# A fused decoder layer on one core: the turn of the attention output one sequence later, and two new orders at the ends of stages

## The reference

```python
x = x + attn(layernorm(x), W_qkv)                 # one head, causal
x = x + xattn(layernorm(x), ctx, mask, Wq..bo)    # 16 heads of 8, softmax over 128 keys
x = x + ffn(layernorm(x), w_gate, w_up, w_down)   # hidden width 384
# act_qdq(t): scale = max(|t|) / 32767 over the WHOLE tensor, t = round(t / scale) * scale
# ffn: x = act_qdq(x); up = act_qdq(x @ dq(w_up).T); gate = act_qdq(x @ dq(w_gate).T)
#      gate = act_qdq(gate * fixed_qdq_u16(sigmoid(gate))); o = act_qdq(gate * up)
#      return o @ dq(w_down).T                    # dq: weights at 4 bits in blocks of 32
```

## Time and profile before

| | us |
|---|---|
| median of 3 runs (lowest, highest) | 330.36 (329.21, 331.45) |
| the profiled execution: its time | 329.18 |
| the same execution: span of the trace | 327.4 |
| PE busy, share of the span | 303.7 (93%) |
| DVE | 273.6 (84%) |
| ACT | 255.3 (78%) |
| POOL | 191.2 (58%) |

### The profile page before, as it was taken

The page is one execution under the profiler, slowest core; times in us unless marked ns, Lnnn a source line. Parts: engine busy times, 40 slices in busy tenths (PEclk is TensorE's granted clock), DMA queues, the critical chain, the costliest instruction groups (busy, mean ns, idle before and its releaser), DMA issues.

```text
span 327.4 us, 9964 instructions
## 1 busy us (share of the span) xinstructions
PE 303.7 (93%) x3757; PEld 208.7 (64%) x3757; DVE 273.6 (84%) x652; ACT 255.3 (78%) x470; POOL 191.2 (58%) x339
## 2 busy tenths in 40 slices
PE   6999999997999999999999998999966689697996
PEld 5787877886566666666666666844322254357996
DVE  5489988777888989999999975877789996989754
ACT  3578888986798998899899896797787758992940
POOL 3679999971348797866857578100077773781000
PEclk9999999999999999999999999999999999999999
DMA  6941366642203565500000000000000000000134
GB/s 167 292 124 33 99 207 194 206 129 72 68 2 100 161 183 163 149 2 6 4 3 4 3 4 2 1 0 0 2 0 1 0 1 2 0 0 1 36 98 126
DMA packets 23754, 21.65 MB, mean 66 GB/s; under 512 B 3577, under 2 KB 21530, under 8 KB 23706
## 3 DMA queue, kind: packets, MB, share of 16 engines
q1 hardware_dynamic: 22170, 20.73, 21.0%
q10 hardware_dynamic: 1536, 0.28, 0.5%
HBM read 14.70 MB, written 6.30 MB: 64 GB/s over the span
## 4 chain that ended last, share of the span: by engine, by line
PE 66%; DVE 11%; ACT 9%; POOL 6%; issue 4%; DMA 2%; SPq 1%; POOLq 0%; ACTq 0%; DVEq 0%
PE banks L772 11%; PE banks L716 9%; PE banks L992 8%; DVE mxs L1823 7%; PE banks L1062 7%; PE banks L646 4%; PE banks L794 4%; PE banks L785 3%; PE banks L639 3%; ACT ng L1358 3%; PE banks L790 3%; PE banks L725 2%; POOL rstd L380 2%; PE banks L709 2%; PE banks L658 2%
## 5 line engine op out<-in xcount | busy, mean ns | idle before, releaser
L1597 DVE TENSOR_REDUCE nm<-banks 128x4 f32<-128x512 f32 x128 | 83.2, 682 | 7.2 <-PE banks L716 5.8
L1261 ACT ACTIVATE PT<-banks,bmask,vmask 128x1024 f32<-128x1024 f32 x64 | 76.6, 1199 | 0.0
L992 PE MATMUL banks<-X3T,upT 128*128 128x512 f32 x96 | 44.3, 601 | 11.5 <-DVE mxs L1823 8.9
L577 POOL TENSOR_TENSOR G<-ng,sq 128x1536 int32<-128x1536 int32 (+3 forms) x10 | 27.9, 2791 | 36.4 <-DVE sq L1854 36.4
L1823 DVE TENSOR_REDUCE mxs<-G 128x1 f32<-128x1536 int32 (+3 forms) x30 | 42.2, 1425 | 4.3 <-ACT G L1319 3.8
L772 PE MATMUL banks<-PT,VP 128*32 128x128 f32 x1024 | 41.2, 279 | 0.0
L716 PE MATMUL banks<-kd,qd 32*128 32x128 f16 x512 | 37.9, 217 | 2.0 <-ACT pT L1133 1.6
L992 PEld LDWEIGHTS banks<-X3T,upT 128*128 128x128 f32 x96 | 17.4, 191 | 34.2 <-issue 15.8
L716 PEld LDWEIGHTS banks<-kd,qd 32*128 32x128 f16 x512 | 22.7, 92 | 18.7 <-issue 7.8
L1103 ACT ACTIVATE h<-X,shift,rstd 128x128 f32<-128x128 f32 x64 | 26.3, 484 | 7.2 <-POOL shift L425 7.2
L772 PEld LDWEIGHTS banks<-PT,VP 128*32 128x32 f32 x1024 | 24.0, 109 | 9.8 <-issue 3.0
(11 more groups left out here) (200 smaller groups left out, 740.1 us busy)
## 6 DMA issues: line engine op xcount, KB each, us to landing
kd<-k_dram SPq DMA_DIRECT2D x32, 128.0 KB, 2.6
qd<-q_dram SPq DMA_DIRECT2D x32, 128.0 KB, 2.7
ctxg<-in_ctx_dram SPq DMA_DIRECT2D x8, 256.0 KB, 3.0
out_dram<-y SPq DMA_DIRECT2D x7, 256.0 KB, 2.3
X<-in_x_dram SPq DMA_DIRECT2D x3, 512.0 KB, 7.1
X3T<-m_dram SPq DMA_DIRECT2D x1, 896.0 KB, 5.9
k_dram<-khi SPq DMA_DIRECT2D x7, 128.0 KB, 1.9
k_dram<-klo SPq DMA_DIRECT2D x7, 128.0 KB, 2.0
```

Source lines behind the costliest of these rows:

```text
L577: nc.gpsimd.tensor_tensor(GI[:, c], ng[:, u, part], sq[:, u, part], ALU.mult).then_inc(S["b_t"], 1)
L992: m = pe.matmul(bank(2 + FC * (g % 2) + k), w[:, k * P:k * P + P], grp(X3T, g), start=True, stop=True)
L1261: act.activation(PT[:, a, :], bank(2 + 2 * a, 2), ACT.Exp, bias=bmask[:, n:n + 1], scale=vmask[:, n:n + 1]).then_inc(S["t_exp"], 1)
L1597: V.tensor_reduce(nm[:, n % 2, c:c + NSET], bank(u).rearrange("p (h m) -> p h m", m=P), AX.X, ALU.max, negate=True).then_inc(S["t_max"], 1)
```

## The change

Three things at once:

1. In cross attention, `turn` and `project` of a sequence run one round later, for sequences up to 26 (LATE): in round n, `turn(n-2)` stands between `max_rows(n+1)` and `queries(n-1)`, and `project(n-2)` where `project(n-1)` stood. Their outputs go to the bank of the following sequence (`late_bank`). ACT copies accordingly (`turn_copy(n-2)`, with a new wait until `attend(n-1)` is over, and `project_copy(n-3)`), POOL adds and DVE takes statistics one round later, and `aggregate3` moves from b = 1 to b = 2. Round 28 does both the late and the ordinary turn and projection; rounds 29 to 31 are as before.
2. At its end, DVE does `attend(30)` and `attend(31)` before the aggregates, maxima and statistics that stood ahead of them, and PE turns the output of 31 before the third group of rows.
3. In the fourth pass group 6 is shared at 1024 instead of 768; POOL also makes the second block of group 7's product; DVE takes the largest of group 5 before its product of 6, and the largest of the last two groups in the order in which products arrive.

```diff
+LATE = B - GB - 2
...
-            return PB if g < UW or g == NG - 2 else 2 * GT
+            return PB if g < UW else 2 * GT
...
+        def late_bank(n):
+            return bank(6 + (n + 1) % 2 if n <= LATE else 6 + n % 2)
...
@@ POOL, round n
-                if 1 < n < B - 1:
+                if 2 < n <= LATE + 3:
+                    add_rows(n - 3)
+                if LATE + 2 < n < B - 1:
                     add_rows(n - 2)
@@ POOL, last group's product
-            pool.wait_ge(S["c_un"], up_made(NG - 2) + 2)
-            nc.gpsimd.tensor_tensor(GI[:, g * FW:g * FW + GT], tn[:, g % 2, 0:GT], un[g % 3][:, 0:GT], ALU.mult
-                                    ).then_inc(S["c_op"], 1)
+            for k in range(2):
+                pool.wait_ge(S["c_un"], up_made(NG - 2) + 2 + k)
+                nc.gpsimd.tensor_tensor(GI[:, g * FW + k * GT:g * FW + (k + 1) * GT], tn[:, g % 2, k * GT:(k + 1) * GT],
+                                        un[g % 3][:, k * GT:(k + 1) * GT], ALU.mult).then_inc(S["c_op"], 1)
@@ PE, cross(n)
                     max_rows(n + 1)
+                if 1 < n <= LATE + 2:
+                    pe.wait_ge(S["t_ou"], n)
+                    turn(n - 2)
                 if n > 0:
                     queries(n - 1)
...
-                elif n > 1:
+                elif n > LATE + 2:
                     pe.wait_ge(S["t_wc"], n - 1)
+                elif n > 2:
+                    pe.wait_ge(S["t_wc"], n - 2)
                 pv(n, 0)
...
                 second_half_bank(n, 0)
-                if n > 0:
+                if n == LATE + 2:
+                    project(n - 2)
+                if n > LATE + 1:
                     turn(n - 1)
...
-                if 0 < n and n != B - 2:
+                if 1 < n < LATE + 2:
+                    project(n - 2)
+                elif n > LATE + 1 and n != B - 2:
                     project(n - 1)
@@ PE, after the rounds
-            for g in range(3):
+            for g in range(2):
                 turn_early_rows3(g)
             turn(B - 1)
+            turn_early_rows3(2)
@@ PE, fourth pass
-            for name, value, k in (("c_tn", NG, 6), ("c_tn", NG + 1, 4), ("c_op", NG - 1, 4), ("c_op", NG, 4), ("c_od", NG + 1, 6)):
+            for name, value, k in (("c_tn", NG, 6), ("c_tn", NG + 1, 4), ("c_op", NG - 1, 4), ("c_od", NG, 4), ("c_op", NG, 4), ("c_op", NG + 1, 6)):
@@ ACT
             def turn_copy(n):
                 act.wait_ge(S["t_oT"], n + 1)
+                if n <= LATE:
+                    act.wait_ge(S["t_o"], n + 2)
...
             for n in range(2, B):
                 probs(n, 0)
                 out_copy(n - 1)
-                if n < B - 1:
+                if 2 < n <= LATE + 2:
+                    project_copy(n - 3)
+                elif LATE + 2 < n < B - 1:
                     project_copy(n - 2)
                 if n + 1 < B:
                     max_copy(n + 1)
+                if n == LATE + 2:
+                    turn_copy(n - 2)
                 probs(n, 1)
-                turn_copy(n - 1)
+                if n < LATE + 2:
+                    turn_copy(n - 2)
+                if n == LATE + 2:
+                    act.wait_ge(S["t_oT"], n)
+                    project_copy(n - 2)
+                if n > LATE + 1:
+                    turn_copy(n - 1)
...
-            up_levels(NG - 1, slice(0, GT))
-            up_levels_in_place(NG - 1, slice(GT, 2 * GT))
+            for k in range(2):
+                up_levels(NG - 1, slice(k * GT, (k + 1) * GT))
@@ DVE, cross attention and its end
-                if 1 < n < B - 1:
+                if 2 < n <= LATE + 3:
+                    stat3(n - 3)
+                if LATE + 2 < n < B - 1:
                     stat3(n - 2)
-                if g > 0 and b == 1:
+                if g > 0 and b == (2 if g < NG - 1 else 1):
                     aggregate3(g - 1)
...
+            attend(B - 2)
             aggregate3_last(0, 2)
             largest3(NG - 3, 2 * NG - 5, (2, 4))
-            attend(B - 2)
             largest3(NG - 2, 2 * NG - 4, (0, GB))
             residual(B - 2)
+            attend(B - 1)
             stat3(B - 2)
             aggregate3_last(2, 3)
-            attend(B - 1)
             rows3_copy(2, 2)
@@ DVE, fourth pass
             for g in range(NG - 1):
+                if g == NG - 2:
+                    product_largest(g - 1, g - 1, slice(0, FW))
                 product(g, slice(product_split(g), FW))
-                if g > 0:
+                if 0 < g < NG - 2:
                     product_largest(g - 1, g - 1, slice(0, FW))
             g = NG - 1
-            product_largest(g - 1, g - 1, slice(PB, FW))
-            product_largest(g - 1, g, slice(0, PB))
-            for k, c in enumerate((slice(2 * GT, FW), slice(GT, 2 * GT))):
-                product(g, c)
-            product_largest(g, g + 1, slice(0, FW))
+            product_largest(g - 1, g - 1, slice(2 * GT, FW))
+            product(g, slice(2 * GT, FW))
+            product_largest(g - 1, g, slice(0, 2 * GT))
+            product_largest(g, g + 1, slice(2 * GT, FW))
+            for k in range(2):
+                product_largest(g, g + 2 + k, slice(k * GT, (k + 1) * GT))
```

More of the change, by code:

```diff
@@ L244, in decoder, with turned, projected @@
         X4 = X[:, :].rearrange("p (b d) -> p b d", d=P)
+        def late_bank(n):
+            return bank(6 + (n + 1) % 2 if n <= LATE else 6 + n % 2)
+        def turned(n):
+            return late_bank(n)[:, 0:P]
+        def projected(n):
+            return late_bank(n)[:, P:2 * P]
         def live(g):
@@ L789, in turn @@
                 pe.wait_ge(S["t_o"], n + 1)
-                pe.transpose(bank(6 + n % 2)[:, 0:P], on_[:, :], ident[:, :]).then_inc(S["t_oT"], 1)
+                pe.transpose(turned(n), on_[:, :], ident[:, :]).then_inc(S["t_oT"], 1)
             def project(n):
                 pe.wait_ge(S["t_oTc"], n + 1)
-                pe.matmul(bank(6 + n % 2)[:, P:2 * P], oT[:, :], WXT[:, 3, :], start=True, stop=True).then_inc(S["t_wo"], 1)
+                pe.matmul(projected(n), oT[:, :], WXT[:, 3, :], start=True, stop=True).then_inc(S["t_wo"], 1)
             for i in range(NG - 1):
@@ L1243, in turn_copy @@
                 act.wait_ge(S["t_oT"], n + 1)
+                if n <= LATE:
+                    act.wait_ge(S["t_o"], n + 2)
                 wait(act, "t_wo", n)
-                act.activation(oT[:, :], bank(6 + n % 2)[:, 0:P], ACT.Copy).then_inc(S["t_oTc"], 1)
+                act.activation(oT[:, :], turned(n), ACT.Copy).then_inc(S["t_oTc"], 1)
             def project_copy(n):
@@ L1250, in project_copy @@
                     act.wait_ge(S["t_x2"], n - 1)
-                act.activation(wo[:, n % 2, :], bank(6 + n % 2)[:, P:2 * P], ACT.Copy).then_inc(S["t_wc"], 1)
+                act.activation(wo[:, n % 2, :], projected(n), ACT.Copy).then_inc(S["t_wc"], 1)
             def rows3_copy(n, g):
@@ L1276, in _ @@
             probs(1, 1)
-            turn_copy(0)
             for n in range(2, B):
@@ L1900, in _ @@
             for g in range(NG - 1):
+                if g == NG - 2:
+                    dve.wait_ge(S["c_op"], g)
+                    dve.wait_ge(S["c_od"], g)
+                    product_largest(g - 1, g - 1, slice(0, FW))
                 dve.wait_ge(S["c_un"], up_made(g) - (g >= UW))
@@ L1912, in _ @@
             dve.wait_ge(S["c_od"], NG - 1)
-            product_largest(g - 1, g - 1, slice(PB, FW))
+            product_largest(g - 1, g - 1, slice(2 * GT, FW))
+            dve.wait_ge(S["c_tn"], NG + 1)
+            dve.wait_ge(S["c_un"], up_made(NG - 2) + 1)
+            product(g, slice(2 * GT, FW))
             dve.wait_ge(S["c_op"], NG - 1)
-            product_largest(g - 1, g, slice(0, PB))
-            dve.wait_ge(S["c_tn"], NG + 1)
-            for k, c in enumerate((slice(2 * GT, FW), slice(GT, 2 * GT))):
-                dve.wait_ge(S["c_un"], up_made(NG - 2) + 1 + 2 * k)
-                product(g, c)
-            dve.wait_ge(S["c_op"], NG)
-            dve.wait_ge(S["c_od"], NG + 1)
-            product_largest(g, g + 1, slice(0, FW))
-            dve.wait_ge(S["c_mx"], NG + 1)
+            product_largest(g - 1, g, slice(0, 2 * GT))
+            dve.wait_ge(S["c_od"], NG)
+            product_largest(g, g + 1, slice(2 * GT, FW))
+            for k in range(2):
+                dve.wait_ge(S["c_op"], NG + k)
+                product_largest(g, g + 2 + k, slice(k * GT, (k + 1) * GT))
+            dve.wait_ge(S["c_mx"], NG + 3)
             dve.wait_ge(S["g_guard"], 8)
```

## The result

The kernel after the change takes 325.80 us (median of 8 runs, 325.04 to 328.14), the kernel before, on the same chip, 329.88 (8 runs, 329.21 to 331.45). The ratio is 0.9878, with an interval from 0.9851 to 0.9905: 1.2% faster, about 4.1 us. The profiled execution took 325.96, with a span of 324.2.

A forecast was written before the change was run, and what follows sets the result against it. Cross attention: PE, ACT and DVE nearly full, an ACT-PE-ACT loop as long as PE's order; DVE bounds the fourth pass's end. 329.18 - 1.6 - 0.38 + 0.71 - 0.16 - 1.42 = 326.3, on the median 327.5; range 325.0 to 330.2.

The forecast's parts named there:

- rival B: Cross attention rounds: no lag from the aggregate, DVE catching up inside its two banks; 3.9 us saved, median 325.2; chance 0.17.
- round 28: Seam round with turn and project both twice: 4.27 us instead of 3.56, +0.71; bounds +0.5 and +1.2.
- The light round: Cross attention round without the aggregate's lag: 3.43 us instead of 3.565, saving 0.135 in each of 26 rounds.
- If ACT is ready: Condition for PE's gain of 0.15 us a round: ACT's probs ends at 1.65, leaving 0.09 for the release.
- rival A: Cross attention rounds: release after probs takes 0.24 us, so the period stays 3.565; median 329.8; chance 0.22.
- The aggregate's lag: Aggregate at b = 2 makes DVE late where the following round has a largest3: 0.38 us lost, five times, 1.9.
- The new wait: ACT's turn_copy waits for attend(n-1) in cross attention: cost zero, up to 0.5 us a group if the lag grows.
- Round 1: First seam round, lacking turn and project: -0.38 us from the 3.62 it took.
- The end of cross attention: turn(30) comes 0.40 us earlier, of which the chain keeps -0.16; bounds 0 and -0.4.
- The fourth pass: New DVE order and POOL's pieces at its end: last maximum at 298.66 against 300.08, -1.42 us; bounds -0.9 and -1.6.
- Rival D: New end of the fourth pass gives nothing, for instance because POOL is late; 328.9 us on the median; chance 0.05.
- PE's filling products end before the last maximum: End of the fourth pass: PE's filling products would be over before DVE's last maximum; no time was charged for them.

The follow-up runs named there:

- e5: Kernel after with one more unit-matrix transpose per round, beside the late turn; 326.93 us, ratio 0.9939 to the kernel before.
- e4: Kernel after with ACT's turn_copy held until PE has made the round's scores, the turn keeping its new place; 329.18 us, ratio 0.9961 to the kernel before.
- e6: Kernel after with one more unit-matrix transpose per round, in the turn's old place ahead of pv(n,1); 327.87 us, ratio 0.9947 to the kernel before.
- e7: Kernel after with aggregate3 of groups 0 to 4 at b = 3 instead of 2, some POOL work moved too; 324.13 us, ratio 0.9833 to the kernel before.
- e8: e7 with three filling products instead of six after the fourth pass's last product; 324.29 us, ratio 0.9848 to the kernel before.
- e3: Kernel before with only the third part of the change, the new end of the fourth pass; 329.03 us, ratio 0.9962.
- e1: Kernel before with only the first part of the change, the late turn and projection with all that follows them; 328.15 us, ratio 0.9930.
- e2: Kernel before with only the second part of the change, the new order at the end of cross attention; 329.33 us, ratio 0.9988.

## Why the prediction was right, and where it was off

**The sign and the size of the whole** came out: 327.5 forecast (-0.87%), 325.8 measured (-1.22%, interval -0.95 to -1.49), inside the range of 325.0 to 330.2. It fell below 327.06, where the prediction had put rival B and a part of the forecast's own spread with 0.35, and not within one per cent of before, to which it gave 0.61. The mechanism was that of the forecast, not that of B: the lag is there, even larger. That the sum came so near is in part luck. The rounds gave 2.1 more than forecast by one term, and four things took 1.3 of it back: a larger lag (0.3), round 9 (0.5), small delays in some rounds (0.3) and round 28 (0.2).

**The light round**: 3.35 instead of 3.43, the term that was mis-sized. By the prediction's own words ("one below 3.40, would make it wrong") its account of the light round is wrong. The failed step is "New PE times: `queries` 0.24, `pv(n,0)` 0.61, keys 1.19". It added the turn's 0.11 to a stretch in which PE had time to spare. In the earlier trace rows `queries` starts at 0.13 and 0.06 behind `oun`; the prediction read this row for the length of a release and didn't ask what it says of PE: that PE had come early. In the trace of after the turn stands there, `pv(n,0)` stays at 0.50 and the keys at 1.07. With the keys that early, DVE's bound on the second keys, which the prediction took to decide the round, is no longer what PE waits for, and ACT's `probs` decides instead: `pv(n,1)` at 1.69, not 1.74. 26 rounds at 0.215 instead of 0.135 are 5.6 instead of 3.5. e5, in which PE really has the 0.11 more, runs at 3.44.

**"If ACT is ready"**: it is, and e4 shows that the gain hangs on it. `probs` ends and `pv(n,1)` starts 0.06 later (135.50 + 1.20, 136.76). The 0.09 that the prediction left for the release were enough, and rival A is out; e6 says the same from the other side, since there the 0.26 remain without ACT.

**The aggregate's lag**: 0.44 in five rounds (3.79 against 3.35), forecast 0.38, and at the rounds and by the mechanism that the prediction gave: `attend` late, reductions late, PE waiting for the bank. e7 shows it by moving it. Together 2.2 instead of 1.9, and some 0.03 in the rounds with the aggregate itself.

**Not forecast**: round 9 (+0.5). "POOL has the same work" was right, down to the time it takes (6.33 and 6.35). What was missed is when it begins: `roots3` stayed in its round while the aggregate for which it waits moved one round on, and the rounds around it got shorter while POOL's work did not. So the rounds: -5.6 + 2.2 + 0.5, and 0.3 in rounds 2, 7, 10 and those with an aggregate, is -2.6 (-2.51 in the table).

**The new wait**: "cost zero, up to 0.5 a group if the lag passes that". Zero in the ordinary rounds; ACT doesn't idle there, since `attend` is over at 136.38 and `probs` only at 136.70. But in **round 28**, where `turn_copy(26)` stands ahead of `probs`, the prediction had costed only PE's added work and the second turn. It left this wait out there, and had 0.71 for 0.94; its upper bound of 1.2, put down to a wait for DVE at the second turn, covers it.

**Round 1**: -0.38, exact. **The end of cross attention**: turn(30) 0.42 earlier (forecast 0.40), of which the chain keeps 0.33, not 0.16: the copy of the third group came 0.29 earlier, so it depended less on turn(31) than "four transposes" behind it made it.

**The fourth pass**: -1.48 (forecast -1.42), DVE's sequence as written down, POOL's pieces each in time. Rival D is out. "PE's filling products end before the last maximum" was wrong: by the model of their ends they end 0.7 behind its end, and they cost about 0.24, as e8's trace shows; it is most of the +0.2 in the last line of the table, so the part nets about -1.2, which is what e3's ratio says (0.38% of 330).

## What to carry to other kernels

When an instruction is moved into a stretch, look first whether its engine idled there, by the start of the next instruction against its releaser's end, and not by the "busy" share: here the 0.11 us of the turn vanished in front of `pv(n,0)`, in time that no row named idle. A full engine and a loop through two engines look alike in the table; the loop shows only when one follows who releases whom until the same instruction comes again one round later. When a loop and an engine's own order are nearly of one length, as here 3.56 and 3.54, expect nothing from shortening one of them. And when steps move by one round, check on every queue what stayed at fixed n and waits for something that moved, and at the seam between the two orders each wait again, with what now stands behind it.

## What was not expected of the hardware

The granted clock falls now and then in stretches in which the work is the same. Two rows, the first of the kernel after in the feed-forward layer, the second of e7 before cross attention:

```profile
245.00:255.00 10.00, 8.56 (x17) 2.97 (x15) 10.00 (x7) 7.60 (x6) 8.21 (x3) 0.83 0.00 1
```

```profile
0.00:88.00 88.00, 82.05 (x553) 65.13 (x555) 69.15 (x249) 64.32 (x180) 61.11 (x105) 0.98 0.47 142
```

In the first, at 0.83 where the kernel before has 1.00, DVE is busy all 10 us, and the stretch takes as long as before (82.16 and 82.15 between the same two points): PE had time to spare.

In the second what matters is where the fall lies. In e7 it is in the last part before cross attention (0.96 from 70 to 80 us, 0.84 from 80 to 88), and the first `max_rows` comes at 85.77, 1.1 us later than in the kernel after, where nothing was changed. All six traces with a fall there (e1, e2, e4, e6, e7, e8) have this `max_rows` at 85.5 to 85.9; the four without it (before, after, e3, e5) at 83.9 to 84.6. e3 shows 0.98 over the first 88 us as well, but with its fall in the first 20 us (0.92 and 0.91), and it is not late. What sets the falls off, no run shows. So two profiled spans can differ by as much as a whole part of this change, and the account has to be made between points that both traces have.
